# A cross-attention and expert-mixture kernel: weight splits spread over the last batch, rows of batch 4 split earlier, the last stage's first routing moved ahead

## What is computed

```python
x = x + xattn(layernorm(x), ctx, ctx, attn_bias, mask, in_proj_w, in_proj_b, out_proj_w, out_proj_b)
# ffn(layernorm(x)):
d2 = x2 + p2[None, :] - 2.0 * (xf @ prototypes.T)
w = softmax(-sqrt(max(d2, 0)) / max(abs(temp), 0.1))
topw, topi = top_k(w, 2); topw = topw / sum(topw)
out = sum over the two: topw * (A[idx] @ (B[idx] @ xf) + bias[idx])
```

## Time and profile before

| what | us |
|---|---|
| median of 3 runs | 877.52 (875.0 to 877.64) |
| the profiled execution | 875.95 |
| its span, first to last instruction | 873.7 |
| PE busy | 843.1 (96%) |
| VectorE busy | 619.2 (71%) |
| ScalarE busy | 503.0 (58%) |
| GpSimd busy | 183.5 (21%) |

### The profile page before, as it was taken

One profiled execution on the slowest core, in us unless ns is written; L12 is line 12 of the kernel. 1 busy time (PEld: TensorE's weight loads), 2 busy tenths in 40 slices (PEclk: granted clock), 3 DMA queues, 4 the chain that ended last, 5 costly groups with the idle time before them and its releaser, 6 DMA issues.

```text
span 873.7 us, 20514 instructions
## 1 busy us (share of the span) xinstructions
PE 843.1 (96%) x8000; PEld 747.2 (86%) x8000; DVE 619.2 (71%) x1458; ACT 503.0 (58%) x1065; POOL 183.5 (21%) x237
## 2 busy tenths in 40 slices
PE   7999999999999999999999999999989987999998
PEld 4878889888888989898889988889978876888886
DVE  6676676677667766776677667777757668886874
ACT  4346656666666566656666665567756653444563
POOL 1041112011201120112121111210267536320000
PEclk9999999999999999999999999999999999999999
DMA  8886655665475747574757475555588322110011
GB/s 260 280 183 150 153 146 128 165 155 146 111 185 135 169 107 188 142 171 103 185 143 175 100 199 135 147 135 136 136 227 197 103 76 65 57 58 30 22 43 43
DMA packets 80481, 119.87 MB, mean 137 GB/s; under 512 B 8517, under 2 KB 59789, under 8 KB 80386
## 3 DMA queue, kind: packets, MB, share of 16 engines
q1 hardware_dynamic: 78402, 111.75, 50.5%
q0 software_dynamic: 1984, 6.82, 2.6%
HBM read 79.25 MB, written 39.28 MB: 136 GB/s over the span
## 4 chain that ended last, share of the span: by engine, by line
PE 77%; ACT 5%; issue 5%; DVE 5%; DMA 5%; POOL 2%; SPq 1%; DVEq 0%; POOLq 0%
PE prob_ps L1030 15%; PE acc L966 13%; PE h_ps L1552 10%; PE out_ps L1045 8%; PE acc L957 8%; PE score_ps L1017 5%; PE score_ps L1021 4%; PE acc L974 3%; DVE score_sb L807 3%; PE big L1552 3%; ACT score_sb L626 2%; PE acc L994 2%; ACT probs_sb L635 1%; PE out_ps L1054 1%; PE dot_ps L1552 1%
## 5 line engine op out<-in xcount | busy, mean ns | idle before, releaser
L626 ACT ACTIVATE score_sb<-score_sb,neg_max 112x750 f32<-112x750 f32 x256 | 236.2, 923 | 71.1 <-DVE neg_max L807 68.0
L807 DVE CUSTOM_DVE_ANT_0 score_sb<-score_ps,neg_bias 112x750 f32<-112x750 f32 x256 | 239.4, 935 | 42.7 <-PE score_ps L1021 36.6
L1030 PEld LDWEIGHTS prob_ps<-ident,score_sb 112*125 112x125 f32 x1536 | 235.2, 188 | 19.4 <-issue 1.8
L1030 PE MATMUL prob_ps<-ident,score_sb 112*125 112x112 f32 x1536 | 246.0, 269 | 2.3 <-issue 1.4
L635 ACT ACTIVATE probs_sb<-prob_ps 125x336 f32<-125x336 f32 x256 | 114.9, 449 | 189.6 <-PE prob_ps L1030 187.6
L817 DVE COPY probs_sb<-prob_ps 125x336 f32<-125x336 f32 x256 | 129.1, 504 | 118.8 <-PE prob_ps L1030 117.5
L1017 PE MATMUL score_ps<-k_st,q_st 97*112 97x512 f32 x256 | 105.0, 410 | 2.2 <-DMA q_st<-q_parts 1.7
L517 POOL COPY rsum_wide<-rsum 112x256 f32<-112x256 f32 x32 | 12.7, 397 | 373.6 <-DVE rsum L826 373.6
L966 PE MATMUL acc<-w_hi,ctx_hi 128*125 128x512 f32 x192 | 88.6, 461 | 0.0
L957 PE MATMUL acc<-ctx_hi,w_hi 128*128 128x374 f32 (+1 forms) x240 | 86.1, 359 | 0.2 <-DVE kq_parts L709 0.2
L957 PE MATMUL acc<-ctx_lo,w_hi 128*128 128x374 f32 (+1 forms) x240 | 85.6, 357 | 0.0
(11 more groups left out here) (191 smaller groups left out, 1574.7 us busy)
## 6 DMA issues: line engine op xcount, KB each, us to landing
k_st<-k_parts SPq DMA_DIRECT2D x96, 375.0 KB
k_parts<-kq_parts SPq DMA_DIRECT2D x60, 188.0 KB, 2.4
k_parts<-kq_parts SPq DMA_DIRECT2D x60, 187.0 KB, 4.4
q_st<-q_parts SPq DMA_DIRECT2D x96, 112.0 KB
ctx_raw<-in_ctx_t SPq DMA_DIRECT2D x14, 752.0 KB, 6.5
q_parts<-kq_parts SPq DMA_DIRECT2D x30, 224.0 KB, 2.3
xb<-in_x SPq DMA_DIRECT2D x8, 448.0 KB, 5.3
attn_t<-attn SPq DMA_DIRECT2D x32, 112.0 KB, 1.9
```

What stands on the lines that cost most here:

```text
L626: nc.scalar.activation(scores[:, w % NSC, :], scores[:, w % NSC, :], ACT.Exp, bias=neg_max[:, w % UB:w % UB + 1], scale=-1.0, accum_out=su ...
L807: nc.vector.tensor_tensor_reduce(out=scores[:, w % NSC, :], in0=score_ps[:, at:at + S], in1=neg_bias[:, w // HG % TC, :], scale=1.0, scala ...
L1030: last = nc.tensor.transpose(prob_ps[j][0:SW, s * TW:(s + 1) * TW], scores[:, w % NSC, (BT * j + s) * SW:(BT * j + s + 1) * SW], ident[0:T ...
```

## The change

It has four parts.

- **Chunks.** `CHUNKS_AT` is spread: two chunks stay in batch 6 (units 28 and 30), the other ten go to units 2, 4, 9, 10, 14, 15, 18, 21, 23 and 27 of batch 7 (the last was at unit 18).
- **Rows.** The rows of x are loaded apart from the attended rows, straight into one of two buffers (`xbs`: `xb`, and the old input buffer `x_res`), and the bias is added in place. The units of splits and biases are shifted, and a fifth split (batch 4, unit 29) is done in `weave`, into the buffers of `ctx_hi[0]` and `ctx_lo[0]`, which `finish` now also uses, in turn with `at_hi` and `at_lo`. `finish` adds the bias for batch 4 and then loads, splits and biases batches 5 to 7. A split now needs the projection two batches back, and the one of batch 5 also waits for the first routing (`route_st_ready`).
- **Order of the last stage.** VectorE does the temperature first, the routing of batch 0 right after its distances, then the experts' bias, then `normalise(1)`. ACT widens the routes before its second `copy_h`. PE projects the two halves of batch 4 with one `down` between them.
- **Expert bias.** Its four loads are issued by ACT at the top of `finish` in place of SP; ACT makes two of the four pieces, VectorE two; PE waits for them only at its last product of the batch (`bst_split`). The temperature has its own semaphore.

```diff
-CHUNKS_AT = (28, 29, 30, 31, UB + 1, UB + 2, UB + 3, UB + 9, UB + 10, UB + 13, UB + 17, UB + 18)
+CHUNKS_AT = (28, 30, UB + 2, UB + 4, UB + 9, UB + 10, UB + 14, UB + 15, UB + 18, UB + 21, UB + 23, UB + 27)
-SPLITS_AT = {5: 0, 11: 1, 19: 2, 26: 3}
-BIASES_AT = {7: 0, 15: 1, 22: 2, 29: 3}
-ATTENDED_AT = {2: 0, 9: 1, 17: 2, 24: 3}
+SPLITS_AT = {5: 0, 11: 1, 19: 2, 24: 3, 29: 4}
+BIASES_AT = {7: 0, 13: 1, 20: 2, 26: 3}
+ROWS_AT = {2: 0, 9: 1, 17: 2, 24: 3, 31: 4}
+ATTENDED_AT = {2: 0, 9: 1, 17: 2, 22: 3, 27: 4}
...
+        self.at_part = [(cut(self.ctx_hi_first, 0, [P, KT, T]), cut(self.ctx_lo_first, 0, [P, KT, T])),
+                        (self.at_hi, self.at_lo)]
+        self.xbs = [self.xb, self.x_res]
...
                     else:
                         eng.wait_ge(sh.at_ready, n)
-                        eng.wait_ge(sh.xb_ready, n)
...
+                if b == B - 1 and u in ROWS_AT:
+                    n = ROWS_AT[u]
+                    if n == 0:
+                        eng.wait_ge(xt_ps_ready, TC * B)
+                    if n >= 2:
+                        eng.wait_ge(sh.x1_ready, TC * (n - 1))
+                    load_rows(eng, sh.xbs[n % 2], x, n, sh.xr_loaded[n % 2])
...
-                        eng.wait_ge(xt_ps_ready, TC * B)
-                    else:
-                        eng.wait_ge(sh.x1_ready, TC * n)
-                    add_output_bias(eng, sh, sh.xr_loaded, n + 1)
+                    add_output_bias(eng, sh, sh.xbs[n % 2], sh.xr_loaded[n % 2], n // 2 + 1)
...
             def load(b):
                 eng.wait_ge(at_ready, b)
-                eng.wait_ge(xb_ready, b)
-                load_attended(eng, sh, x, attn_t, b, at_more_loaded, xr_more_loaded)
+                load_attended(eng, sh, attn_t, b, at_more_loaded)
+                eng.wait_ge(x1_ready, TC * (b - 1))
+                load_rows(eng, xbs[b % 2], x, b, xr_more_loaded[b % 2])
 
             def split(b):
-                eng.wait_ge(o_ready, TC * b)
+                eng.wait_ge(o_ready, TC * (b - 1))
                 eng.wait_ge(y2_ready, b - EARLY)
-                split_attended(eng, sh, (at_hi, at_lo), at_more_loaded, b - EARLY, b, passed)
-                eng.wait_ge(x1_ready, TC * b)
-                add_output_bias(eng, sh, xr_more_loaded, b - EARLY)
-
+                if b == EARLY + 2:
+                    eng.wait_ge(route_st_ready, 2)
+                split_attended(eng, sh, at_part[b % 2], at_more_loaded, b - EARLY - 1, b, passed)
+                add_output_bias(eng, sh, xbs[b % 2], xr_more_loaded[b % 2], (b - EARLY - 2) // 2 + 1)
+
+            add_output_bias(eng, sh, xbs[(EARLY + 1) % 2], sh.xr_loaded[(EARLY + 1) % 2], (EARLY + 1) // 2 + 1)
             for p in range(2):
                 eng.wait_ge(sh.attn_stored[p], 1 + 16 * B * NG // 2)
-            for b in range(EARLY + 1, B):
+            for b in range(EARLY + 2, B):
...
# ScalarE
+            for r in range(4):
+                eng.dma_start(bst_raw[r * NP:(r + 1) * NP, :], f_bias).then_inc(small_loaded, 16)
             norm(0)
...
             nc.scalar.activation(bst_hi[:, :], bst_raw[:, :], ACT.Copy).then_inc(bst_ready, 1)
+            for r in (0, 2):
+                rows = slice(r * NP, (r + 1) * NP)
+                nc.scalar.activation(bst[rows, :], bst_raw[rows, :], ACT.Copy).then_inc(bst_split, 1)
             distance_root(0)
             eng.wait_ge(small_ready, 1)
             second_weight(0)
             copy_h(0, 0)
+            widen_route(0)
             copy_h(0, 1)
-            widen_route(0)
             norm(1)
# VectorE
             small_first()
+            temperature()
             norm(1)
             residual(EARLY, 0)
             residual(EARLY, 1)
             eng.wait_ge(p2_ready, 1)
             routing_dot(0)
+            routing(0)
+            expert_bias()
             normalise(1)
-            small_later()
-            routing(0)
             residual(EARLY + 1, 0)
+            routing_weights(0)
             residual(EARLY + 1, 1)
-            routing_weights(0)
             yt_low(1)
# TensorE
-            for c in range(TC):
-                project_out(EARLY + 1, c)
+            project_out(EARLY + 1, 0)
             down(0, 0, 1)
+            project_out(EARLY + 1, 1)
             down(0, 1, 0)
             down(0, 1, 1)
             transpose_y(1)
-            eng.wait_ge(small_ready, 1)
```

More of the change, by code:

```diff
@@ L206, in __init__ @@
         self.x1_first = cut(self.v_first, 0, [TW, EARLY * TC, E])
+        self.ctx_hi_first = sb("ctx_hi_first", [P, KT, HC], F32R)
+        self.ctx_lo_first = sb("ctx_lo_first", [P, KT, HC], F32R)
         self.at_hi = sb("at_hi", [P, KT, T], F32R)
@@ L211, in __init__ @@
         self.xb = sb("xb", [TW, TC, E])
+        self.at_part = [(cut(self.ctx_hi_first, 0, [P, KT, T]), cut(self.ctx_lo_first, 0, [P, KT, T])),
+                        (self.at_hi, self.at_lo)]
+        self.xbs = [self.xb, self.x_res]
         self.at_loaded = ctx.enter_context(nc.semaphore("at_loaded"))
-        self.xr_loaded = ctx.enter_context(nc.semaphore("xr_loaded"))
+        self.xr_loaded = [ctx.enter_context(nc.semaphore(f"xr_loaded{p}")) for p in range(2)]
         self.bo_loaded = ctx.enter_context(nc.semaphore("bo_loaded"))
@@ L237, in split_attended, with add_output_bias @@
     eng.tensor_tensor(lo[:, :, :], sh.at_in, hi[:, :, :].bitcast(F32), ALU.subtract).then_inc(sh.at_ready, 1)
-def add_output_bias(eng, sh, xr_loaded, loads):
+def add_output_bias(eng, sh, xb, xr_loaded, loads):
     eng.wait_ge(xr_loaded, 16 * loads)
     for c in range(TC):
-        last = eng.tensor_tensor(sh.xb[:, c, :], sh.x_res[:, c, :], sh.bo_row[:, :], ALU.add)
+        last = eng.tensor_tensor(xb[:, c, :], xb[:, c, :], sh.bo_row[:, :], ALU.add)
     last.then_inc(sh.xb_ready, 1)
@@ L265, in weave @@
         MROW = NBLK * D
-        ctx_hi = [sb(f"ctx_hi{f}", [P, KT, HC], F32R) for f in range(2)]
-        ctx_lo = [sb(f"ctx_lo{f}", [P, KT, HC], F32R) for f in range(2)]
-        at_part = [(cut(ctx_hi[0], 0, [P, KT, T]), cut(ctx_lo[0], 0, [P, KT, T])), (sh.at_hi, sh.at_lo)]
+        ctx_hi = [sh.ctx_hi_first, sb("ctx_hi_second", [P, KT, HC], F32R)]
+        ctx_lo = [sh.ctx_lo_first, sb("ctx_lo_second", [P, KT, HC], F32R)]
+        at_part = sh.at_part
         k_st = [sb(f"k_st{p}", [MROW + 1, HG, S], F32R) for p in range(2)]
@@ L1129, in finish @@
         iota = sb("iota", [TW, NP])
-        ident, w_hi, w_lo, at_hi, at_lo, xb = sh.ident, sh.w_hi, sh.w_lo, sh.at_hi, sh.at_lo, sh.xb
+        ident, w_hi, w_lo, at_part, xbs = sh.ident, sh.w_hi, sh.w_lo, sh.at_part, sh.xbs
         at_ready, xb_ready = sh.at_ready, sh.xb_ready
@@ L1172, in finish @@
         small_loaded = sem("small_loaded")
+        temp_loaded = sem("temp_loaded")
         bst_ready = sem("bst_ready")
+        bst_split = sem("bst_split")
         small_step = sem("small_step")
@@ L1179, in finish @@
         at_more_loaded = sem("at_more_loaded")
-        xr_more_loaded = sem("xr_more_loaded")
+        xr_more_loaded = [sem(f"xr_more_loaded{p}") for p in range(2)]
         iota_ready = sem("iota_ready")
@@ L1230, in _ @@
             eng.dma_start(protos_sb[:, :], protos).then_inc(protos_loaded, 16)
-            for r in range(4):
-                eng.dma_start(bst_raw[r * NP:(r + 1) * NP, :], f_bias).then_inc(small_loaded, 16)
-            eng.dma_start(temp_col[:, :], temp.partition_broadcast(TW)).then_inc(small_loaded, 16)
+            eng.dma_start(temp_col[:, :], temp.partition_broadcast(TW)).then_inc(temp_loaded, 16)
             for b in range(B):
@@ L1360, in small_first, with temperature @@
                     .then_inc(pt_ready, 1)
[L1362 to L1371, removed]
+            def temperature():
+                eng.wait_ge(temp_loaded, 16)
                 nc.vector.tensor_scalar(t_neg[:, :], temp_col[:, :], -1.0, 0.1, ALU.mult, ALU.max)\
@@ L1379, in small_later, with expert_bias @@
                 eng.wait_ge(iota_ready, 1)
+            def expert_bias():
+                eng.wait_ge(bst_ready, 1)
+                for r in (1, 3):
+                    rows = slice(r * NP, (r + 1) * NP)
+                    nc.vector.tensor_tensor(bst[rows, :], bst_raw[rows, :], bst_hi[rows, :].bitcast(F32),
+                                            ALU.subtract).then_inc(bst_split, 1)
             def residual(b, c):
@@ L1384, in residual @@
                 eng.wait_ge(o_ready, TC * b + c + 1)
-                nc.vector.tensor_tensor(x1_of(b)[:, c, :], big[c][0:TW, :], xb[:, c, :], ALU.add)\
+                nc.vector.tensor_tensor(x1_of(b)[:, c, :], big[c][0:TW, :], xbs[b % 2][:, c, :], ALU.add)\
                     .then_inc(x1_ready, 1)
@@ L1566, in project_out @@
                     eng.wait_ge(gated_ready, b - EARLY - 1)
-                three_passes(big[c][0:TW, :], lambda a, k: (at_hi, at_lo)[a][:, k, c * TW:(c + 1) * TW], w_of(0), NG)\
```

(2 more changed lines are left out.)

11 lines of the change are left out of this document (6 added, 5 removed).

## The result

The changed kernel takes 873.03 us (median of six executions) against 877.4 us of the kernel before, measured beside it: ratio 0.9945, 95% interval 0.9924 to 0.9966. One of the six was disturbed (1198.65 us) and is left out of the ratio. By that ratio it is 4.8 us faster (4.4 by the two medians), where 10.0 were forecast: the direction held, the size was half, and the median lies above the range of 864.5 to 871.5. The profiled execution took 868.3 us with a span of 866.3, 7.4 us under the span of before.

The account below looks back on a forecast made before the run. PE, busy 843.1 of 873.7 us, was taken as the bound, so only its stalls could yield: 2.9 us in batch 7 plus 7.1 in the last stage, 10.0 in all, from 877.5 to 867.5 us; range 864.5 to 871.5.

Parts of the forecast that it names:

- Chunks, 2.9 us: Batch 7: with chunks spread, the widened row sums come at about 637.3 and PE's wait goes, gaining 2.9 us.
- These moves I cost at nothing: Batch 7: the other chunks move later by up to ten units, at no cost, covered by POOL's idle time.
- Rows and the fifth split: Batch 7: extra loads and split fit at cost 0, and buy the 1.07 us PE waited for `at_lo`.
- a rival for a gain: "More goes": PE's 1.43 us stop at 683.48 may vanish with the loads placed otherwise; 866.1 us, chance 0.12.
- And with it the half clock: Last stage: the 5.1 us gap before `transpose_routes` goes and the 1.2 GHz clock behind it, 1.9 us of the gain.
- a wait of 2.9 us in batch 7 left the clock alone: Argument against the slower-front rival (870.5 us, chance 0.2), in which two short gaps make the clock fall, another 1.9 us.
- The front of the last stage: Four ACT issues cost 1.9 us; `dot` at 724.9 against 723.88, yet PE projects batch 4 0.7 us earlier.
- Routing first: Last stage: routing ahead of `normalise(1)` ends at 733.7 against 741.28, so PE's 5.1 us gap goes.
- 1.9 holds: Last stage: `normalise(1)` takes VectorE 1.9 us, since POOL's next split waits for the routing and POOL is quiet.
- The split of batch 5 in time: Last stage: the split starts at 733.8, takes 3.1 us and is ready at 736.9, with 1.8 to spare.
- The signs: Checks on PE's waits, clock and last-stage times; the forecast falls if the span shrinks by less than 6.7 us.
- its rivals: Slower front 0.2, batch 7 stall only moves 0.08, more goes 0.12, slower 0.05; times 870.5, 870.4, 866.1, about 880.

Follow-up runs that it names:

- before_again: The kernel before, unedited, profiled a second time: one execution, 877.38 us.
- e7: The kernel before with only SP's two loads for batch 2 held until the row sums of the group at 681 us: 877.08 us, ratio 0.9999.
- e2: The changed kernel with the old `CHUNKS_AT` list, all else as changed: 875.88 us, ratio 0.997 against the kernel before.
- the held kernel: The changed kernel with SP's two loads for batch 2 held until the row sums near 679 us, run twice: 869.57 and 869.21 us.
- e3: First run of the changed kernel with both loads of batch 2 held until the row sums near 679 us: 869.57 us, ratio 0.9925.
- e4: The changed kernel with VectorE's old order in the last stage: 872.45 us, ratio 0.9943 against the kernel before.
- e5: The changed kernel, the split of batch 5 no longer held for the routing of batch 0: 876.88 us, ratio 0.9987 against the kernel before.
- e9: The changed kernel, batch 2's attended rows loaded at unit 12 instead of 17, only its rows of x held: 869.3 us, ratio 0.9913.

## Why the prediction was wrong, point by point

- **Chunks, 2.9 us.** Right in kind: the wait is gone in every profile with the new list, and what was late next was not a chunk. The size is that of one profile: with the old list it is 2.9, 2.5 and 2.4 us in three profiles (before, before_again, e7). "These moves I cost at nothing" held in so far as the old list leaves the stop near 680 at 3.3 us (e2).
- **Rows and the fifth split, "Cost 0 here".** This is the step that failed. I asked only whether the fifth split fits and its load lands in time. That the new rules for SP also move the loads of batch 2 stands nowhere in the prediction, so their price was put at nothing without a reason. PE's stop stood in my own rows, as 1.43 us "for nothing visible, while the load traffic is dense", and I made it a rival for a gain. Dropping the wait for the bias let SP issue batch 2's 896 KB earlier: 8 and 5 us ahead of the stop's start in place of 2.8 and 2.3. The stop grew to 3.3 to 3.5 us in all six profiles that have the change with both loads free, and over the kernels it follows these two loads: 2.7 with one held, 1.6 with one early and one held, 1.1 to 1.3 with both held; 1.4 and 0.4 in the kernel before. Price in a pair of profiles: 1.8 us.
- **"And with it the half clock", 1.9 us.** The fall behind the gap did go. But the mean clock rose by 0.001 and not by 0.004, since falls behind the longer stop took its place: in five of the six profiles with a stop of 3.3 us or more it falls right there. With both loads held the mean is 0.9958. My argument that a wait of 2.9 us in batch 7 left the clock alone held for one profile: behind the same wait it falls in e2's (0.59 for 4 us) and in e7's (0.83 from 640 to 650 us). That part of the loss, some 2.3 us between the changed and the held kernel (871.7 and 869.4 in the median), holds the stop's length and its clock together, less the 1.0 to 1.4 us that the held kernel waits for the split; I can't part them.
- **The front of the last stage.** Right in kind, a little too dear. ACT's four issues took 1.97 us (1.9 forecast). The temperature landed after 3.6 us and not 4.4, before `pt_lo` was done, so `dot` came 9.4 us behind the stage's start against 9.0 forecast, with 1.5 us of the lower clock in it. Without that fall the stage takes 22.6 (e3's profile), and my 23.2 was 0.6 too long. So neither ACT's issues nor the temperature's place explain the miss.
- **Routing first.** The times were right to about one us: normalisation at 0.16 us an operation, the last routing piece at 19.3 us (18.2 forecast, and the clock's fall at the seam lies before it), PE 0.5 us late for `yt_lo` as forecast. The credit was not. VectorE's order is worth 0.7 us (e4); what closed the gap is that POOL has nothing to do meanwhile. The wait for `route_st_ready` alone is worth 3.7 to 4.4 us (e5). What the fifth split adds wasn't run alone, but the kernel before shows its size: between `dot` and the last routing piece VectorE's small operations that ran beside POOL's splits and biases took 6.9 us more in all than the same ones in the changed kernel. I had that as the reason that "1.9 holds", a side remark, where it was the main term.
- **The split of batch 5 in time.** Right: no wait for `at_lo` is left in PE's list.
- **The sum.** 10.0 us against 7.4 between the profiles and 4.8 in the comparison. For the held kernel, which differs by one wait, it is 6.6 to 7.9. Of the 2 to 3 us that are still missing, 1.0 to 1.4 are its wait for the split; the first profile's two waits, longer than in the second by 0.4 and 0.5 us, may be part of the rest. How much of it is clock stays open.
- **The signs.** I had said that the forecast falls if the span shrinks by less than 6.7 us. It shrank by 7.4, and none of the signs against it showed: they watched one profile, the waits I knew and the stage's front, and not the stop.

The range failed for one more reason: its rivals held the stop's change as a gain only, so its upper end had no place for it.

## What to carry to other kernels

When a wait is dropped, list what it had kept apart: here a queue's wait for a bias had kept two transfers from filling the queues ahead of a place where PE is sensitive to traffic. A stop that the profile can't name, with the transfer engines full in that stretch, belongs into the sum with both signs. And where VectorE runs a chain of tiny operations on the critical path, look first at what GpSimd does in those us: here keeping it quiet by one wait was worth some 4 us, the reordering 0.7.

## What the runs showed of the hardware that I had not expected

PE's stop lies at the same place in all 14 profiles, inside one `turn`, where no semaphore is waited for. In the 4 us ahead of its end packets of the two instruction queues move while the transfer engines are nearly full; here the changed kernel, 678 to 681 us:

```profile
DMA  7999999989995995699677967998499957331200
...
q8 instruction: 1, 0.02, 2.3%
q14 instruction: 1, 0.01, 1.0%
```

The packet of q8 tells more. It is the only one of its queue in the 12 us ahead of the stop's end. It begins between 680.5 and 681 in the kernel before, between 679.5 and 680 in the changed one and between 676.5 and 677 in the held one:

```profile
q8 instruction: 1, 0.02, 16.8%
...
q8 instruction: 1, 0.02, 13.9%
...
q8 instruction: 1, 0.02, 14.4%
```

In windows of a quarter of a us its start can be set beside PE's. With the stop of 0.4 us (e7) it begins 2.5 us ahead of the stop, with those of 1.4 (before) and 1.1 us (held) 1.5 ahead, and with that of 3.3 us (changed) 0.8 behind the stop's start. The stop's end comes 2.4 to 3.1 us behind the packet's start in all 14 profiles, 2.6 in most. So PE goes on about the same time after this packet, and what varies is how late it comes. e9's second stop, in another place, fits: a q8 packet begins between 643.5 and 643.75, and PE goes on at 646.13.

It is then very likely the fetch of PE's next instructions, queued behind the loads. That q8 serves PE is inferred; the trace doesn't name the engine.

The time of one and the same program follows its mean granted clock by some 6 to 8 us for 0.01 (8.0 over the 73 executions of the kernel before, 6.2 over the 17 of the changed one). After the stop of 1.9 us at the seam the clock falls in one profile of the kernel before (0.83 from 710 to 720 us) and not in the other. One profile says where it can fall; how often it does, only many executions say.
